# Projecting the last keys of four batches to V in three tiles

## The chip, the cores and the metric

The kernel runs on one core of a Trainium2 chip. Its measure is the device time of one execution in microseconds (us), as a median over runs. Five engines work side by side and wait for each other by semaphores: TensorE (PE in the rows; PEld is its weight load), VectorE (DVE), ScalarE (ACT), GpSimd (POOL) and SyncE (SP, which issues most of the DMAs).

## The reference, cut to what matters

Two layers of gated cross attention, each with a feed-forward part behind it. `ctx_1024` is the context, 8 batches of 722 keys of width 512; `x` has 8 batches of 100 queries. Both layers project the same context to K and V anew:

```python
def _heads(x):                       # 16 heads of 32
    b, s, _ = x.shape
    return x.reshape(b, s, H, W).transpose(0, 2, 1, 3)
q = _heads(x_q @ Wq.T + bq)
k = _heads(x_k @ Wk.T + bk)          # x_k = x_v = ctx_1024
v = _heads(x_v @ Wv.T + bv)
scores = jnp.einsum('bhqw,bhkw->bhqk', q, k) / np.sqrt(W)
...                                  # layer 0 masks keys, layer 1 does not
p = jax.nn.softmax(scores, axis=-1)
h = jnp.einsum('bhqk,bhkw->bhqw', p, v)
```

Layer 1 projects `h` once more by `Wo`. The feed-forward part of layer 0 has four ternary products, that of layer 1 is a quantized gate, up and down.

## The kernel before

**Precision.** Most operands are float32, split into a high part (a cast to `float32r`) and a low part (the rest), so a projection is three matmuls for each of the four blocks of 128 input features: high by high, low by high, high by low (`PAIRS`). Twelve matmuls make one *job*.

**Jobs.** A K job is a group of 128 output features (4 heads) over 384 or 338 keys: `("k", batch, group, half)`. A V job is a tile of 128 keys over all 512 output features: `("v", batch, kt)`. 722 keys are five tiles of 128 and one, `kt` = 5, of 82 rows. That last one is the V tail here.

**The attention loop.** `for i in range(NP)` runs over 64 pairs of heads, 8 for a batch. *Step i* on TensorE is: `scores(i+1)` (four matmuls), `turn(i)` (twelve transposes of the softmax weights), the jobs of `beside(i)`, then `weigh(i-1)`, six matmuls of weights by V. `BESIDE` sets which jobs go beside which of the 8 steps of a batch, mostly for the batch that follows; at i = 8b stand the V tail and the last K half of batch b itself.

**The others in step i.** ScalarE: `high_weighed(i-2)` (copies a part of a weighing out), `high_turned(i)` (three copies), the exponentials `weights(2i+2)` and `weights(2i+3)`, and `high_job`, which rounds a job's bank to the high part. The second exponential stands behind the first job where a step has two, and ahead of it where it has one (`len(beside(i)) < 2`). VectorE: two maxima (`peak`), `low_weighed(i-2)` (three additions), `low_turned(i)` (three subtractions), and `low_job`, which subtracts the high part from the bank. In layer 0 some steps are `early`: there `low_weighed` stands ahead of the maxima. GpSimd makes the low part of the next context (`low_ctx`); ScalarE makes the high part.

**Banks.** Jobs, weighings and a few more items (`inv`, `res`, `xn`, `out`) are written to PSUM banks 5 and 7 in turn. The list `RINGS` has the order; before item r is written, `ring_free` waits until item r-2 has been read: a job by `v_job` (its low part is made), a weighing by `v_fin` (its additions are done).

**K on its way.** High and low part of a K half are staged in `kst`, stored to DRAM (`store_k`) and loaded spread out over partitions (`load_k`). `high_job` of the K half waits until the staging tile of the group before has landed.

Of the kernel before, what the change touches and what calls it, by code (L numbers as in the profile page):

```python
# [6 lines left out]
F32R = mybir.dt.float32r  # L7
# [56 lines left out]
BESIDE = [(("v", 0, 5), ("k", 0, 3, 1)),  # L64
# [9 lines left out]
def beside(i):  # L74

    if i >= NP:
        return []
    return [(j[0], i // 8 + j[1]) + j[2:] for j in BESIDE[i % 8] if i // 8 + j[1] < B]

# [58 lines left out]
for _i in range(NP + 1):  # L138
    for _l in range(2):
        JOBS[_l] += beside(_i)  # L140
        if scaled_at(_i) is not None:
            RINGS[_l].append(("inv", scaled_at(_i)))
# [23 lines left out]
LAST_OF = {(j[1], half_of(j)): i for i, j in enumerate(JOBS[0])}  # L166
# [63 lines left out]
def flamingo_kernel(nc, t, out):  # L230
    top = ExitStack()
    with top:
# [28 lines left out]
        def scol(which, m):  # L261
# [13 lines left out]
        d_row, g_row = sem("d_row"), sem("g_row")  # L275
        d_xo = [sem(f"d_xo{b}") for b in range(B)]
# [24 lines left out]
        g_xf, g_ul, g_wh, g_mask, g_wl, g_rt, g_res, g_mv = (  # L301
            sem("g_" + n) for n in ("xf", "ul", "wh", "mask", "wl", "rt", "res", "mv"))
        g_self, g_nh, g_xr, g_wo, g_ol, g_rq, g_xn, g_xq = (
            sem("g_" + n) for n in ("self", "nh", "xr", "wo", "ol", "rq", "xn", "xq"))
# [15 lines left out]
        for L in range(2):  # L320
# [26 lines left out]
            x = 4 * TOKENS[L][0][1]  # L347
            m.xT = [PT[:, x * c:x * c + x].rearrange("p (k n) -> p k n", k=4) for c in (0, 1)]
# [83 lines left out]
        def job_out(m, j, bank):  # L432
            if j[0] == "k":
                return ps[:, bank, 0:HALF[j[3]][1]]
            return ps[0:KM[j[2]], bank, :]
# [69 lines left out]
        def _(e):  # L505
            w = Waits(e)
            def attention(L):
# [9 lines left out]
                if L == 0:  # L517
# [25 lines left out]
                    spread_q(L, m, 0)  # L543
                    store_k(L, m, *K30[1:])
                    load_ctx(L, m, 1, 0, 3)
                else:
# [22 lines left out]
                    load_k(L, m, 0, 1)  # L569
                    store_k(L, m, *K30[1:])  # L570
                for k in range(4):
                    load_ctx(L, m, 1, 1, k)
                for i in range(NP):
                    b, p = divmod(i, 8)
                    if p in (0, 2):
                        load_k(L, m, b, 2 + p // 2)
                    if L == 0 and p == 3 and b:
# [39 lines left out]
                    if p in (1, 5) and b + 2 < B:  # L617
                        for k in range(4):
# [42 lines left out]
            def load_ctx(L, m, b, half, k):  # L661
# [3 lines left out]
                e.dma_start(m.raw[:, k, off:off + n], t["ctx"][b, k][:, off:off + n]).then_inc(d_ctx[half][k], 16)  # L665

# [94 lines left out]
        def _(e):  # L761
# [13 lines left out]
            def attention(L):  # L775
# [31 lines left out]

                def ring_free(item):
# [1672 lines left out]
```

## Time and profile before

| | us |
|---|---|
| median of 3 runs (1589.46 to 1589.9) | 1589.48 |
| the profiled execution | 1587.91 |
| its span, first to last instruction | 1586.1 |
| TensorE busy | 1571.0 |
| VectorE busy | 1023.3 |
| ScalarE busy | 968.0 |
| GpSimd busy | 400.7 |

The two attention loops run from about 53 to 485 us (layer 0) and from 1056 to 1490 us (layer 1) of the span; between them lies the feed-forward part of layer 0, behind them that of layer 1. The page says how long each engine was busy; a chain of waits says which work ended last, step by step; a timeline has the instructions in order of time. A matmul's duration in a timeline overlaps the next one's, so the cost of a group is read from start to start.

### The profile page before, as it was taken

The page shows a single profiled execution, that of the slowest core. Times are in us where ns is not written, and L with a number is a line of the kernel's source. Part 1 is how long each engine was busy: PE and PEld are TensorE (multiplying, and loading weights), DVE is VectorE, ACT ScalarE, POOL GpSimd, SP SyncE. Part 2 cuts the span into 40 slices and gives each one's busy share as a digit, 9 for nine tenths or more (in the row PEclk, how much of TensorE's full clock was granted, in tenths as well). Part 3 has the DMA queues.
Part 4 walks back from the last instruction along what each step waited for, and adds up shares of the span by engine and source line. Part 5 has one row for each costly group of instructions (what it writes and reads, how often), then busy time and mean ns, then how long its engine had stood idle before and what let it go on. Part 6 is the DMA issues. An engine that isn't in the chain of part 4 may idle for free.

```text
span 1586.1 us, 25797 instructions
## 1 busy us (share of the span) xinstructions
PE 1571.0 (99%) x9370; PEld 1430.5 (90%) x9370; DVE 1023.3 (65%) x1821; ACT 968.0 (61%) x2006; POOL 400.7 (25%) x545
## 2 busy tenths in 40 slices
PE   9999999999999999999999999999999999999999
PEld 7899889989989999999999998889989989998765
DVE  6577787787785562223644425647777777777997
ACT  5666767677665455544544435457667667766676
POOL 4111211212144222222222222311102111113651
PEclk9999999999999999999999999999999999999999
DMA  8766776676572326554375643576676667658500
GB/s 245 181 170 169 184 188 178 156 202 175 144 206 86 104 80 198 175 186 160 108 229 194 220 154 98 177 176 180 153 195 165 162 178 178 178 128 227 179 13 30
DMA packets 146966, 258.15 MB, mean 163 GB/s; under 512 B 40944, under 2 KB 91248, under 8 KB 146701
## 3 DMA queue, kind: packets, MB, share of 16 engines
q1 hardware_dynamic: 146497, 256.10, 57.5%
q8 instruction: 86, 1.41, 0.4%
q14 instruction: 51, 0.42, 0.1%
q10 hardware_dynamic: 332, 0.23, 0.0%
HBM read 187.86 MB, written 58.57 MB: 155 GB/s over the span
## 4 chain that ended last, share of the span: by engine, by line
PE 92%; DVE 5%; ACT 2%; issue 1%; DMA 1%; SPq 0%; POOL 0%; DVEq 0%; ACTq 0%
PE ps L1148 33%; PE ps L802 17%; PE ps L798 15%; PE ps L884 8%; PE ps L862 8%; PE ps L950 2%; PE ps L1082 2%; PE ps L851 2%; PE ps L846 2%; PE ps L1099 1%; PE ps L849 1%; PE ps L850 1%; DVE PT L1295 1%; DVE nmax L1289 1%; ACT P L1806 1%
## 5 line engine op out<-in xcount | busy, mean ns | idle before, releaser
L1148 PE MATMUL ps<-ah_f,wh_f 128*128 128x400 f32 (+1 forms) x1296 | 442.9, 343 | 0.0
L1148 PE MATMUL ps<-al_f,wh_f 128*128 128x400 f32 (+1 forms) x1296 | 442.2, 342 | 0.0
L2165 POOL TENSOR_TENSOR cxl<-raw,cxh 128x384 fp32r<-128x384 f32 (+1 forms) x112 | 105.7, 965 | 613.5 <-ACT cxh L1763 613.5
L1685 DVE TENSOR_TENSOR wl_f<-raw_f,wh_f 128x1024 fp32r<-128x1024 f32 x85 | 103.7, 1223 | 232.4 <-POOL wh_f L2155 232.4
L1148 PEld LDWEIGHTS ps<-al_f,wh_f 128*128 128x128 f32 x1296 | 243.8, 188 | 0.0
L1148 PEld LDWEIGHTS ps<-ah_f,wh_f 128*128 128x128 f32 x1296 | 243.5, 188 | 0.1
L1289 DVE TENSOR_REDUCE nmax<-ps 100x1 f32<-100x722 f32 x256 | 220.7, 903 | 32.0 <-PE ps L850 28.6
L1806 ACT ACTIVATE P<-ps,nmax 100x722 f32<-100x722 f32 x256 | 219.9, 861 | 31.2 <-DVE nmax L1289 30.9
L1818 ACT ACTIVATE PT<-ps 128x400 fp32r<-128x400 f32 x384 | 165.9, 505 | 69.8 <-PE ps L862 68.5
L2083 ACT ACTIVATE raw_f<-wl_f 128x1024 f32<-128x1024 f32 x88 | 93.4, 1062 | 173.6 <-DVE wl_f L1685 173.6
L1295 DVE TENSOR_TENSOR PT<-ps,PT 128x400 fp32r<-128x400 f32 x384 | 196.4, 567 | 4.3 <-ACT PT L1818 1.1
L2155 POOL CAST wh_f<-raw_f 128x1024 fp32r<-128x1024 f32 x85 | 92.3, 1086 | 334.7 <-PE ps L1148 325.5
L798 PE MATMUL ps<-cxh,wkh 128*128 128x338 f32 (+1 forms) x512 | 172.0, 336 | 1.2 <-DVE cxl L1267 0.8
L798 PE MATMUL ps<-cxh,wkl 128*128 128x338 f32 (+1 forms) x512 | 167.8, 328 | 0.0
L798 PE MATMUL ps<-cxl,wkh 128*128 128x338 f32 (+1 forms) x512 | 167.0, 326 | 0.0
L802 PE MATMUL ps<-wvh,cxh 128*128 128x512 f32 (+1 forms) x384 | 159.1, 414 | 0.9 <-DVE V L1277 0.9
L862 PE MATMUL ps<-ident,P 100*128 100x100 f32 (+1 forms) x1536 | 152.9, 249 | 1.3 <-DVE PT L1295 1.3
L862 PEld LDWEIGHTS ps<-ident,P 100*128 100x128 f32 (+1 forms) x1536 | 143.0, 137 | 11.6 <-ACT P L1806 1.5
L884 PE MATMUL ps<-PT,V 128*128 128x400 f32 x720 | 151.0, 345 | 0.7 <-DVE ksl L1277 0.4
L802 PE MATMUL ps<-wvh,cxl 128*128 128x512 f32 (+1 forms) x384 | 151.1, 394 | 0.0
L802 PE MATMUL ps<-wvl,cxh 128*128 128x512 f32 (+1 forms) x384 | 150.7, 392 | 0.0
L1277 DVE SCALAR_TENSOR_TENSOR ksl<-ps,cols,ksh 128x384 fp32r<-128x384 f32 (+1 forms) x120 | 71.0, 592 | 112.1 <-ACT ksh L1774 112.0
(220 smaller groups left out, 2590.6 us busy)
## 6 DMA issues: line engine op xcount, KB each, us to landing
KS<-kd SPq DMA_DIRECT2D x192, 361.0 KB
raw_f<-in_h SPq DMA_DIRECT2D x64, 512.0 KB, 4.5
raw_f<-in_gud SPq DMA_DIRECT2D x48, 512.0 KB, 4.7
raw<-in_ctx SPq DMA_DIRECT2D x64, 192.0 KB, 3.9
raw_f<-in_w SPq DMA_DIRECT2D x24, 512.0 KB, 3.7
kd<-ksh SPq DMA_DIRECT2D x60, 192.0 KB, 2.1
kd<-ksl SPq DMA_DIRECT2D x60, 192.0 KB, 2.4
raw<-in_ctx SPq DMA_DIRECT2D x64, 169.0 KB, 4.3
```

Source lines behind the costliest of these rows:

```text
L798: ins = e.matmul(o, m.wk[x][:, k, 128 * j[2]:128 * j[2] + 128], m.cx[y][:, k, off:off + n], start=(k == 0 and c == 0), stop=(k == 3 and c ...
L802: ins = e.matmul(o, m.cx[y][:, k, 128 * kt:128 * kt + KM[kt]], m.wv[x][:, k, :], start=(k == 0 and c == 0), stop=(k == 3 and c == 2))
L862: ins = e.transpose(ps[0:KM[kt], bank, o:o + S], m.P[0:S, (2 * i + h) % 3, 128 * kt:128 * kt + KM[kt]], ident[0:S, 0:S])
L884: ins = e.matmul(o, m.V[b % 2][0:r, kt, g, 128 * pr:128 * pr + 128], m.PT[0:r, i % 2, :, kt, :], start=(kt == 0), stop=(kt == KT - 1))
L1148: return e.matmul(o, p, q, start=start, stop=stop)
L1289: e.tensor_reduce(m.nmax[0:S, c:c + 1], scores_of(n), AX.X, ALU.max, negate=True).then_inc(v_max, 1)
L1295: e.tensor_tensor(lo, ps[:, bank, 0:400].rearrange("p (k n) -> p k n", k=2), raw32(hi), ALU.subtract).then_inc(v_t, 1)
L1685: e.tensor_tensor(wl[:, z, :], raw[:, r, :], raw32(wh[:, z, :]), ALU.subtract).then_inc(v_ul, 1)
L1806: e.activation(m.P[0:S, n % 3, :], scores_of(n), ACT.Exp, bias=m.nmax[0:S, c:c + 1], accum_out=m.rs[0:S, r:r + 1]).then_inc(a_exp, 1)
L1818: e.activation(m.PT[:, i % 2, 0, 2 * x:2 * x + 2, :], ps[:, bank, 0:400].rearrange("p (k n) -> p k n", k=2), ACT.Copy).then_inc(a_t, 1)
L2083: e.activation(raw[:, r, :], raw32(wl[:, z, :]), ACT.Abs, accum_out=low[:, z, 0:1]).then_inc(a_raw, 1)
L2165: e.tensor_tensor(m.cx[1][:, k, off:off + n], m.raw[:, k, off:off + n], raw32(m.cx[0][:, k, off:off + n]), ALU.subtract).then_inc(g_cx, 1)
```

## The change

The V tails of batches 0, 1, 2, 3 have 4 x 82 = 328 rows. They are now put into three jobs, of 114, 128 and 114 rows, and those of batches 4 to 7 likewise: keys 0 to 81 of batch 0 and 64 to 81 of batch 1; keys 0 to 63 of batches 1 and 2; keys 64 to 81 of batch 2 and 0 to 81 of batch 3 (`PIECES`; the 18 rows stand at partition 96). The input for such a job is a new array, `ctxt`, that the host lays out (zeros where no key stands). It is loaded into a part of the tile of the raw context (for batch 0 elsewhere) and split to high and low by GpSimd (`split_tail`). The job of batches 0, 1, 2 (and 4, 5, 6) stands at step 8b behind `weigh(i-1)`; at steps 24 and 56 there is none. Its eviction is two pieces on ScalarE and two on VectorE in step 8b+1. `load_ctx(b+2)` of the first half now waits for the job.

```diff
-BESIDE = [(("v", 0, 5), ("k", 0, 3, 1)),
+BESIDE = [(("k", 0, 3, 1),),
...
+def tail_at(i):
+    return i // 8 if i < NP and i % 8 == 0 and i // 8 % 4 < 3 else None
+PIECES = (((0, 0, 0, 82), (96, 1, 64, 82)),
+          ((0, 0, 0, 64), (64, 1, 0, 64)),
+          ((96, 0, 64, 82), (0, 1, 0, 82)))
+TAIL_ROWS = (114, 128, 114)
...
+            JOBS[_l].append(("v", tail_at(_i), KT - 1))      # after beside(_i)
...
             RINGS[_l].append(("pv", _i - 1))
+        if tail_at(_i) is not None:
+            RINGS[_l].append(("v", tail_at(_i), KT - 1))
...
+            m.tail = [[x[:, k:k + 2, 0:256] for k in (2, 0)]
+                      for x in (at(f"tail{i}_{L}", place, shape, F32R) for i, (place, shape) in enumerate(ends))]
...
+                    if p == 7 and tail_at(i + 1) is not None:          # SyncE
+                        load_tail(L, m, b + 1)
...
                     if p in (1, 5) and b + 2 < B:
+                        if p == 1 and b:
+                            w.wait_ge(p_job, tail_done(L, b))
...
+            def load_tail(L, m, b):
+                if b:
+                    wait_ctx(w, L, b + 1, 0, 1)
+                else:
+                    w.wait_ge(p_xt, 8 * L + len(IN[L]))
+                e.dma_start(m.tail_raw[min(b, 1)], t["ctxt"][tail_of(b)].rearrange("p (a n) -> p a n", a=2)).then_inc(d_tail, 16)
...
+                def tail_job(b):                                        # TensorE
+                    j = ("v", b, KT - 1)
+                    ring_free(j)
+                    w.wait_ge(g_tail, 2 * (6 * L + tail_of(b)) + 2)
+                    r, o = TAIL_ROWS[b % 4], job_out(m, j, ring_bank(L, j))
+                    for k in range(4):
+                        wait_low_w(w, L, 4 + k)
+                        n = 128 * (k % 2)
+                        for c, (x, y) in enumerate(PAIRS):
+                            ins = e.matmul(o, m.tail[min(b, 1)][y][:, k // 2, n:n + r], m.wv[x][:, k, :],
+                                           start=(k == 0 and c == 0), stop=(k == 3 and c == 2))
+                    ins.then_inc(p_job, 1)
...
                     if i:
                         weigh(i - 1)
+                    if tail_at(i) is not None:
+                        tail_job(tail_at(i))
...
+                def low_tail(b):                                        # VectorE
+                    j = ("v", b, KT - 1)
+                    w.wait_ge(a_job, NJOB * L + JOB[L][j] + 1)
+                    for v, o in tail_parts(m, b, ring_bank(L, j)):
+                        ins = e.tensor_tensor(v[:, :, 1:3, :], o, raw32(v[:, :, 0:4:3, :]), ALU.subtract)
+                    ins.then_inc(v_job, 1)
...
                     if i >= 2 and not early and not between and (L == 0 or i < NP):
                         low_weighed(i - 2)
+                    if i and tail_at(i - 1) is not None:
+                        low_tail(tail_at(i - 1))
...
                     if i >= 2:                                          # ScalarE
                         high_weighed(i - 2)
+                    if i and tail_at(i - 1) is not None:
+                        high_tail(tail_at(i - 1))
...
+                def split_tail(b):                                      # GpSimd
+                    (high, low), new = m.tail[min(b, 1)], m.tail_raw[min(b, 1)]
+                    w.wait_ge(d_tail, 16 * (6 * L + tail_of(b) + 1))
+                    if b:
+                        wait_ctx(w, L, b + 1, 0, 3)
+                    e.tensor_copy(high, new).then_inc(g_tail, 1)
+                    w.wait_ge(g_tail, 2 * (6 * L + tail_of(b)) + 1)
+                    e.tensor_tensor(low, new, raw32(high), ALU.subtract).then_inc(g_tail, 1)
```

TensorE, layer 1, batch 1: from the end of the K half in step 8 (L798, after it L848) into step 9, before. L884 and L948 are the weighing, L846 to L851 and L910 to L915 the scores, L862 and L926 the transposes, L802 and L852 the V projection of the next batch, L868 the tail's job:

```order
L798 MATMUL ps<-cxh_74,wkl_84 128x338
L884 MATMUL ps<-PT_89,V_1_85 128x400 x6
L846 MATMUL ps<-KS_91,QS_88 100x512
L849 MATMUL ps<-KS_91,QS_88 100x210
L850 MATMUL ps<-KS_91,QS_88 100x210
L851 MATMUL ps<-KS_91,QS_88 100x512
L862 MATMUL ps<-ident,P_78 128x100 x10
L862 MATMUL ps<-ident,P_78 82x100 x2
L802 MATMUL ps<-wvh_76,cxh_74 128x512
```

and with the change:

```order
L848 MATMUL ps<-cxh_78,wkl_88 128x338
L948 MATMUL ps<-PT_93,V_1_89 128x400 x6
L868 MATMUL ps<-wvh_80,tail_1_103 128x512 x2
L868 MATMUL ps<-wvl_81,tail_1_103 128x512
L868 MATMUL ps<-wvh_80,tail_1_103 128x512 x2
L868 MATMUL ps<-wvl_81,tail_1_103 128x512
L868 MATMUL ps<-wvh_80,tail_1_103 128x512 x2
L868 MATMUL ps<-wvl_81,tail_1_103 128x512
L868 MATMUL ps<-wvh_80,tail_1_103 128x512 x2
L868 MATMUL ps<-wvl_81,tail_1_103 128x512
L910 MATMUL ps<-KS_95,QS_92 100x512
L913 MATMUL ps<-KS_95,QS_92 100x210
```

The tail came in behind the weighing and ahead of the scores. What the next V projection waits for, at its first matmul, before:

```order
L862 MATMUL ps<-ident,P_78 128x100 [waits v_t]
L862 MATMUL ps<-ident,P_78 128x100
L862 MATMUL ps<-ident,P_78 82x100 x2
L802 MATMUL ps<-wvh_76,cxh_74 128x512 [waits g_cx,v_job]
L802 MATMUL ps<-wvh_76,cxl_75 128x512
```

and with the change:

```order
L926 MATMUL ps<-ident,P_82 128x100 [waits v_t]
L926 MATMUL ps<-ident,P_82 128x100
L926 MATMUL ps<-ident,P_82 82x100 x2
L852 MATMUL ps<-wvh_80,cxh_78 128x512 [waits g_cx,v_fin]
L852 MATMUL ps<-wvh_80,cxl_79 128x512
```

`v_job` (a job's low part) has become `v_fin` (the additions of a weighing). ScalarE in step 8 of the same batch and the start of step 9, before. `sum` is `high_weighed`, `PT` is `high_turned`, `P,rs` an exponential, `V` and `ksh` the evictions of a V job and a K half:

```order
L1833 ACTIVATE sum_90<-ps 64x200 [waits v_fin,p_pv]
L1818 ACTIVATE PT_89<-ps 128x2x200 [waits p_t] x3
L1806 ACTIVATE P_78,rs_81<-ps,nmax_82 100x722 [waits v_max]
L1787 ACTIVATE V_1_86<-ps 82x4x2x64 [waits p_job]
L1806 ACTIVATE P_78,rs_81<-ps,nmax_82 100x722
L1774 ACTIVATE ksh_96<-ps,cols 128x338 [waits d_kd12,p_job]
L1833 ACTIVATE sum_90<-ps 64x200 [waits v_fin,p_pv]
```

and with the change:

```order
L1924 ACTIVATE sum_94<-ps 64x200 [waits v_fin,p_pv]
L1909 ACTIVATE PT_93<-ps 128x2x200 [waits p_t] x3
L1897 ACTIVATE P_82,rs_85<-ps,nmax_86 100x722 [waits v_max]
L1897 ACTIVATE P_82,rs_85<-ps,nmax_86 100x722
L1850 ACTIVATE ksh_100<-ps,cols 128x338 [waits d_kd12,p_job]
L1924 ACTIVATE sum_94<-ps 64x200 [waits v_fin,p_pv]
L1878 ACTIVATE V_1_89<-ps 18x4x2x64 [waits p_job]
L1878 ACTIVATE V_1_90<-ps 82x4x2x64
```

The K half's eviction now stands behind both exponentials, and the tail's two pieces ahead of the copies of step 9. VectorE, the end of step 8 and step 9, before. `nmax` is a maximum, `sum` and `QT` the additions of a weighing, `PT` the three subtractions, `ksl` and `V` low parts:

```order
L1295 TENSOR_TENSOR PT_89<-ps,PT_89 128x2x200 [waits a_t] x3
L1281 TENSOR_TENSOR V_1_86<-ps,V_1_86 82x4x128 [waits a_job]
L1277 SCALAR_TENSOR_TENSOR ksl_97<-ps,cols,ksh_96 128x338 [waits a_job]
L1289 TENSOR_REDUCE nmax_82<-ps 100x1 [waits a_exp,p_sc] x2
L1310 TENSOR_TENSOR sum_90<-ps,sum_90 64x200 [waits a_pv]
L1314 TENSOR_TENSOR QT_93<-ps,sum_90 32x100 [waits v_self]
L1314 TENSOR_TENSOR QT_93<-ps,sum_90 32x100
L1295 TENSOR_TENSOR PT_89<-ps,PT_89 128x2x200 [waits a_t] x3
```

and with the change:

```order
L1369 TENSOR_TENSOR PT_93<-ps,PT_93 128x2x200 [waits a_t] x3
L1343 SCALAR_TENSOR_TENSOR ksl_101<-ps,cols,ksh_100 128x338 [waits a_job]
L1363 TENSOR_REDUCE nmax_86<-ps 100x1 [waits a_exp,p_sc] x2
L1384 TENSOR_TENSOR sum_94<-ps,sum_94 64x200 [waits a_pv]
L1388 TENSOR_TENSOR QT_97<-ps,sum_94 32x100 [waits v_self]
L1388 TENSOR_TENSOR QT_97<-ps,sum_94 32x100
L1355 TENSOR_TENSOR V_1_89<-ps,V_1_89 18x4x128 [waits a_job]
L1355 TENSOR_TENSOR V_1_90<-ps,V_1_90 82x4x128
L1369 TENSOR_TENSOR PT_93<-ps,PT_93 128x2x200 [waits a_t] x3
```

The tail's two low parts stand behind the maxima and the additions.

## Rows read from the trace of the kernel before

**Rows 1.** Page before, parts 1 and 2: TensorE busy, its granted clock
```profile
PE 1571.0 (99%) x9370; PEld 1430.5 (90%) x9370; DVE 1023.3 (65%) x1821; ACT 968.0 (61%) x2006; POOL 400.7 (25%) x545
...
PEclk9999999999999999999999999999999999999999
```

**Rows 2.** Waits of TensorE: who, for whom, us, times, longest
```profile
PE ps L802 <- DVE V L1277: 0.9, 1, 0.9
```

**Rows 3.** Chain of waits, layer 1, steps 8 and 9: start, us, what
```profile
1117.74 2.77 PE ps L802 x12
1120.51 1.86 PE ps L798 x12
1122.38 1.09 PE ps L884 x6
...
1125.15 2.80 PE ps L802 x12
```

**Rows 4.** Timeline, layer 1, TensorE: start, us, engine, line, operation, out<-in
```profile
1115.89 0.40 PE L846 MATMUL ps<-KS,QS 96*100 96x512 f32 x1
...
1123.31 0.39 PE L846 MATMUL ps<-KS,QS 96*100 96x512 f32 x1
...
1124.93 0.48 PE L802 MATMUL ps<-wvh,cxh 128*128 128x512 f32 x1
```

**Rows 5.** The same timeline, ScalarE
```profile
1118.28 0.86 ACT L1806 ACTIVATE P<-ps,nmax 100x722 f32<-100x722 f32 x1
...
1122.41 0.54 ACT L1774 ACTIVATE ksh<-ps,cols 128x338 fp32r<-128x338 f32 x1 [0.43 <-PE ps L798]
...
1125.69 0.87 ACT L1806 ACTIVATE P<-ps,nmax 100x722 f32<-100x722 f32 x1
...
1127.29 0.20 ACT L1806 ACTIVATION_READ_ACCUMULATOR P<-ps,nmax 100x1 f32 x1
```

**Rows 6.** The same timeline, VectorE
```profile
1116.52 1.73 DVE L1289 TENSOR_REDUCE nmax<-ps 100x1 f32<-100x722 f32 x2
1118.16 0.35 DVE L1310 TENSOR_TENSOR sum<-ps,sum 64x200 f32<-64x200 f32 x1
...
1119.13 1.54 DVE L1295 TENSOR_TENSOR PT<-ps,PT 128x400 fp32r<-128x400 f32 x3
1121.18 0.69 DVE L1281 TENSOR_TENSOR V<-ps,V 82x512 fp32r<-82x512 f32 x1 [0.51 <-ACT V L1787]
1122.99 0.57 DVE L1277 SCALAR_TENSOR_TENSOR ksl<-ps,cols,ksh 128x338 fp32r<-128x338 f32 x1 [1.13 <-ACT ksh L1774]
...
1126.09 0.54 DVE L1314 TENSOR_TENSOR QT<-ps,sum 32x100 f32<-32x100 f32 x2
```

**Rows 7.** Timelines, TensorE, two weighings: without a wait, after one
```profile
1122.21 1.25 PE L884 MATMUL ps<-PT,V 128*128 128x400 f32 x6
...
211.12 1.36 PE L884 MATMUL ps<-PT,V 128*128 128x400 f32 x6 [0.39 <-DVE ksl L1277]
```

**Rows 8.** Groups by line, GpSimd: xcount | busy us, mean ns | idle before
```profile
L2186 POOL TENSOR_TENSOR wol<-wos,woh 128x512 fp32r<-128x512 f32 x4 | 5.0, 1282 | 0.1
...
L2183 POOL CAST woh<-wos 128x512 fp32r<-128x512 f32 x4 | 2.3, 615 | 7.1 <-PE ps L802 7.1
```

**Rows 9.** Timeline of layer 1, step 8: GpSimd and the queue of SyncE
```profile
1115.07 1.99 POOL L2165 TENSOR_TENSOR cxl<-raw,cxh 128x384 fp32r<-128x384 f32 x2 [4.46 <-ACT cxh L1763]
...
1119.07 1.27 SPq L693 DMA_DIRECT2D KS<-kd  x3
```

**Rows 10.** Timeline, layer 0, step 33, TensorE
```profile
289.45 0.39 PE L846 MATMUL ps<-KS,QS 98*100 98x512 f32 x1
...
291.43 0.47 PE L802 MATMUL ps<-wvh,cxh 128*128 128x512 f32 x1
```

**Rows 11.** Timeline, layer 0, step 56, VectorE
```profile
455.38 0.54 DVE L1409 TENSOR_SCALAR x<-x,mv,rq 100x512 f32<-100x512 f32 x1
```

**Rows 12.** Chain of waits in order of time, layer 0, step 57
```profile
458.76 0.91 DVE nmax L1289
```

More of the change, by code:

```diff
@@ L151 @@
             RINGS[_l].append(("pv", _i - 1))
+        if tail_at(_i) is not None:
+            RINGS[_l].append(("v", tail_at(_i), KT - 1))
 for _l in range(2):
@@ L162, in half_of @@
     return j[3] if j[0] == "k" else j[2] // 3
-LAST_OF = {(j[1], half_of(j)): i for i, j in enumerate(JOBS[0])}
+LAST_OF = {(j[1], half_of(j)): i for i, j in enumerate(JOBS[0]) if j[0] == "k" or j[2] < KT - 1}
 PLACES = [{i: r for r, i in enumerate(ring)} for ring in RINGS]
@@ L300, in flamingo_kernel @@
         g_ones, g_cx, g_ql, g_rx, g_low, g_tot = (sem("g_" + n) for n in ("ones", "cx", "ql", "rx", "low", "tot"))
[L301 to L304, printed above, removed]
+        g_xf, g_ul, g_wh, g_mask, g_wl, g_rt, g_res, g_set = (
+            sem("g_" + n) for n in ("xf", "ul", "wh", "mask", "wl", "rt", "res", "set"))
+        g_self, g_xr, g_wo, g_ol, g_rq, g_xn, g_xq = (
+            sem("g_" + n) for n in ("self", "xr", "wo", "ol", "rq", "xn", "xq"))
         base = -(-nc.sbuf_base // 32) * 32
@@ L347, in flamingo_kernel @@
             x = 4 * TOKENS[L][0][1]
+            ends = [(o["V1"] + 16384, [128, 4, 256]), (o["raw"], [128, 4, T])]
+            m.tail = [[x[:, k:k + 2, 0:256] for k in (2, 0)]
+                      for x in (at(f"tail{i}_{L}", place, shape, F32R) for i, (place, shape) in enumerate(ends))]
+            m.tail_raw = [at(f"traw{i}_{L}", place, shape)[:, 0:2, 0:256] for i, (place, shape) in enumerate(ends)]
             m.xT = [PT[:, x * c:x * c + x].rearrange("p (k n) -> p k n", k=4) for c in (0, 1)]
@@ L434, in job_out @@
                 return ps[:, bank, 0:HALF[j[3]][1]]
-            return ps[0:KM[j[2]], bank, :]
+            return ps[0:TAIL_ROWS[j[1] % 4] if j[2] == KT - 1 else KM[j[2]], bank, :]
         def ring_bank(L, item):
@@ L474, in rows_of, with tail_done, tail_parts @@
             return x.rearrange("b s d -> (b s) d")[ROW0[n]:ROW0[n] + ROWS[n], :]
+        def tail_done(L, b):
+            return NJOB * L + JOB[L]["v", b - (b % 4 == 3), KT - 1] + 1
+        def tail_parts(m, b, bank):
+            return [(m.V[(b + x) % 2][r0:r1, KT - 1, :, :].rearrange("p g (r n) -> p g r n", r=4),
+                     ps[o:o + r1 - r0, bank, :].rearrange("p (g r n) -> p g r n", g=4, r=2)) for o, x, r0, r1 in PIECES[b % 4]]
         def high_columns(m, j):
@@ L1788, in high_job, with high_tail @@
                                      ACT.Copy).then_inc(a_job, 1)
+                def high_tail(b):
+                    j = ("v", b, KT - 1)
+                    w.wait_ge(p_job, NJOB * L + JOB[L][j] + 1)
+                    w.wait_ge(p_pv, NP * L + 8 * b)
+                    if b == 0:
+                        w.wait_ge(p_xt, 8 * L + len(IN[L]))
+                        w.wait_ge(p_q, 8 * L + 8)
+                        for g in (1, 2):
+                            for h in range(2):
+                                w.wait_ge(d_kd[h][g], kd_done(L, g))
+                    for v, o in tail_parts(m, b, ring_bank(L, j)):
+                        ins = e.activation(v[:, :, 0:4:3, :], o, ACT.Copy)
+                    ins.then_inc(a_job, 1)
                 def high_q(b):
@@ L2341, in attention @@
                     b, p = divmod(i, 8)
+                    if i and tail_at(i) is not None:
+                        split_tail(b)
                     if scaled_at(i + 1) is not None:
@@ L2442, in col @@
         return v.reshape(-1, 128).T
+    tails = np.zeros((6, 128, 4, 128), np.float32)
+    for b in range(B):
+        for o, x, r0, r1 in PIECES[b % 4] if b % 4 < 3 else ():
+            keys = I["ctx_1024"][b + x, 640 + r0:640 + r1, :]
+            tails[tail_of(b), :, :, o:o + r1 - r0] = keys.reshape(r1 - r0, 4, 128).transpose(2, 1, 0)
+    tails = tails.reshape(6, 128, 512)
     a = {
@@ L2446 @@
         "ctx": I["ctx_1024"].transpose(0, 2, 1).reshape(B, 4, 128, T),
+        "ctxt": tails,
         "mask": I["mask_BxS2_ik0"],
```

21 lines of the change are left out of this document (14 added, 7 removed).

## The prediction

> **What bounds the kernel now.** I read the page first: its busy line has TensorE at 99% of the span, and the clock line is full in all forty slices [rows 1]. So a matmul that goes is worth its time, provided that nothing else makes TensorE wait, and a wait that comes is paid in full. The table of waits comes next: projections of context (L802) waited 0.9 us in all the run, once [rows 2]. There is no slack for a gain to hide in. Then the chain of waits in order of time, for what one step of the attention loop is made of. I call step i what TensorE does between the first score matmul of pair i+1 and that of pair i+2; in layer 1, batch 1, step 8 begins at 1115.89 and step 9 at 1123.31 [rows 4]. In step 8 the chain shows the V tail 2.77, the K half 1.86 and the weighing 1.09 [rows 3]; scores and transposes stand before them, and the first job of a step starts 1.62 into it (1124.93 less 1123.31) [rows 4]. The timelines of ScalarE and VectorE come last, because the eviction of a PSUM bank goes through both, and the two banks 5 and 7 are handed out in turn.
>
> **What is removed.** A V projection is twelve matmuls of 512 columns, whether it has 82 or 128 rows: 2.77 against 2.80 [rows 3]. Each layer has eight V tails before and six after (none at steps 24 and 56), so four go: 4 x 2.80 = 11.2 us. Rows 96 to 113 or 64 to 127 of the tile cost TensorE nothing by these two rows.
>
> **What is added off the path.** Twelve loads of 256 KB, a cast and a subtraction of 512 elements on GpSimd each: 0.62 + 1.28 us [rows 8]. GpSimd ends its subtraction for the context at 1117.06 [rows 9], 1.17 into step 8, so the split would end at 3.1. If both took double, because of the strided view, it would be 5.0; TensorE wants it at about 5.4 (below). The load is put into the queue when GpSimd has done the pair before, 4.46 us before 1115.07 [rows 9], and its bytes have nearly six microseconds. I take nothing for it. ScalarE and VectorE get 24 evictions for 16, and they have time: the cost lies in where they stand. The queue of SP is moved too: its load of context b+2 at step 8b+1 now waits for the tail on TensorE, about 8.3 us into step 8b, and behind it stand loads of keys that are used five steps later; nothing.
>
> **What is moved: the first new wait.** Before, step 8b had two jobs, V tail and K half, then the weighing. Now it has the K half, the weighing, and then the tail, which takes the bank that the K half held. TensorE: K half from 1.62 to 3.48, weighing to 4.57. ScalarE: with one job in a step both exponentials stand ahead of the job's eviction. The first begins at 2.39 (1118.28), and the second and its accumulator end 1.80 after such a start (1125.69 to 1127.49), where the next eviction may start about 0.1 earlier [rows 5]: the K eviction runs from 4.1 to 4.6. VectorE has its three subtractions until 4.78 and then the K part of 0.57 [rows 6]: 5.35. With 0.05 for the semaphore the tail can start at 5.40, not 4.57: 0.83. A restart costs more: the weighing that had to wait shows 1.36, one that had not 1.25 [rows 7], so 0.11. First wait 0.94. The second half of the K block before must have landed in DRAM as well, for the staging tile is used again: SP's load that waits for it went out at 1119.07, 3.18 into the step [rows 9], ahead of 4.1, so nothing.
>
> **The second new wait.** The next projection, V of batch b+1 in step 8b+1, takes the bank of weighing 8b-1, which before it did not: there it took that of the K half. VectorE frees this bank by the additions of weighing 8b-1, and they stand in step 8b+1 behind its two maxima. The maxima cannot start before the scores of that step, and these come after the tail. In step 9 the additions ended at 1126.63, 3.32 into the step, and TensorE wants to start the projection at 1.62 [rows 4, 6]. With 0.05 and the restart of 0.11: 3.37 - 1.62 + 0.11 = 1.86. This holds for the five middle places of layer 1 and for batch 1 of layer 0. In layer 0 from batch 2 on, the additions come ahead of the maxima and one more item takes a bank; then the projection wants the bank of the tail, whose two low parts stand behind the maxima. Maxima done at 2.27 (1118.16 less 1115.89; the next begins then), two parts of 0.69 that overlap by 0.05: 3.60; the projection wanted 1.98 (291.43 less 289.45) [rows 6, 10]. 3.65 - 1.98 + 0.11 = 1.78.
>
> **The sum.** Places: batches 1, 2, 4, 5, 6 in two layers, ten. Batch 0 has no weighing ahead and its next projection takes the bank of the K half, so I count nothing there. First waits 10 x 0.94 = 9.4; second waits 6 x 1.86 + 4 x 1.78 = 18.3; together 27.7. From the 11.2 I take what is late next. Step 56 without its tail is 4.6 long: in layer 0 VectorE then has the three subtractions to 4.78, a normalization of 0.54 and K's 0.57 [rows 6, 11], so 5.87, where the maxima could start at 5.23 (0.63 after the scores' start, 1116.52 less 1115.89): 0.6 lost, since from 458.76 on the chain runs over VectorE [rows 12]. Layer 1, without the normalization: 0.1. In layer 0 batch 3, step 25, the additions now start late and the projection with them: 0.3. So 11.2 - 0.6 - 0.1 - 0.3 = 10.2 is left. 27.7 - 10.2 = +17.5 us. The profiled execution took 1587.91, 1.8 more than its span of 1586.1; with the change 1605.4. The median of the runs is 1.57 above that execution: 1607.0.
>
> **Bounds of what is not shown.** A bank wait of this form is not in the trace of before. From below: the first wait could vanish (the K eviction is ready at 3.7, were it taken between the exponentials), which leaves 18.3 - 10.2 = +8.1. From above: each restart as dear as the first matmuls after a wait in the trace, some 0.3 in place of 0.11, and a late landing of the keys: +5, so +22.5. An eviction of 18 partitions lies between nothing and the 0.69 of 82; at nothing the four places of layer 0 would win 0.64 each, -2.6; were it double, +2.8. I take the full 0.69, since the rows of 82 and of 128 partitions agree [rows 6].
>
> A page of the Trainium skill speaks against this change in another way: "TensorE: Matmul & The Clock Gate", section "A second HAM failure mode: psum-queue depth-cycling", says that a TensorE that idles briefly between groups of matmuls, as it cycles through PSUM banks, can swing between its half and its full clock. By that rule the twenty new pauses would also slow what follows them. The row of the trace has the full 2.4 GHz in every slice [rows 1], though with hardly a pause in it, so it cannot decide.
>
> **Rivals.** (A) The waits do not come: the additions and the K part are done in time, so that TensorE finds both banks free. Place: steps 8b and 8b+1; price 0; then -10.2, and the time is 1579.3, faster. It decides for this if the bank of weighing 8b-1 is free at 1.6 into step 8b+1. For it speaks that TensorE waited so little until now; against it the order of VectorE, in which nothing can move the additions ahead of the maxima. Chance 0.09. (B) Only one kind of wait is paid: with the first alone 9.4 - 10.2, 1588.7, no change (0.03); with the second alone +8.1, 1597.6 (0.08). (C) The input of the tail is late at GpSimd or in the queue: TensorE waits for it beyond 5.4; were it 1 us at ten places, 1617.0. The room of 2.3 us speaks against it. Chance 0.06. (D) The clock drops to 1.2 GHz in the pauses. Were one projection of 2.80 after each of ten places at half speed, that is +28: 1635.0. Chance 0.03. The forecast keeps 0.71.
>
> **Numbers.** A measurement here can tell 0.2%, 3.2 us, from no change. Slower: 0.71 + 0.08 + 0.06 + 0.03 = 0.88; same 0.03; faster 0.09. Forecast 1607.0, its own range 1601 to 1612 by the bounds; down to 1597 to take in the second kind alone, up to 1614 for part of (C).
>
> **What would show it.** In the profile after: the idle time before the first matmul of a tail about 0.8 us, ended by VectorE's K part (L1343); before the projection of step 8b+1 about 1.8 us, ended in layer 1 by the additions (L1388), in layer 0 from batch 2 on by the low tail (L1355); steps 8b and 8b+1 together 15.8 us in layer 1 where they were 13.0; steps 24 and 56 shortened to about 4.6; TensorE at 97%. The forecast is wrong if TensorE shows none of these, or if step 24 is not shorter, or if the split on GpSimd ends later than 5.4.

## The result and the profile after

The median went from 1589.47 us to 1609.03 us (1608.46 to 1609.52): a ratio of 1.0123, with a 95% interval of 1.0111 to 1.0135. The change made the kernel 19.6 us slower, where 17.5 were forecast. The profiled execution took 1608.54 us, with a span of 1606.1; it stands against 1587.91 and 1586.1 before. The first lines of the page after:

```profile
PE 1567.9 (98%) x9322; PEld 1430.4 (89%) x9322; DVE 1027.6 (64%) x1829; ACT 970.4 (60%) x2014; POOL 423.9 (26%) x569
...
PE 85%; DVE 8%; issue 2%; DMA 2%; ACT 1%; SPq 1%; POOL 0%; DVEq 0%; ACTq 0%
```

48 matmuls fewer, four tails of twelve, and TensorE's busy time fell by 3.1 us only, while the span grew by 20 [rows 1]. The second line is the chain that ended last: VectorE's share in it is 8%, where it was 5% before. The table of TensorE's waits names the place, where before the projections (now L852, then L802) had waited 0.9 us [rows 2]. Its columns are engine, line and releaser, then us in all, times, the longest:

```profile
PE ps L852 <- DVE QT L1388: 9.2, 6, 1.5
PE ps L852 <- DVE V L1355: 6.5, 4, 1.6
PE ps L868 <- DVE ksl L1343: 4.7, 10, 0.5
PE ps L1063 <- POOL otl L2294: 1.8, 2, 1.6
```

The first three rows came six, four and ten times, each with the releaser that the prediction named: 20.4 us of idle. The steps of the same twenty places grow by more, 25.9 us (table below): a matmul's end in the profile is modelled, so that a part of each wait counts as busy, and a tail takes a little longer in its new place (see the first wait, below). The timeline of layer 1, batch 1, shows both waits. Step 8 begins at 1127.93 and step 9 at 1136.10. First the engines that free the bank of the K half, then the tail (L868), then step 9:

```profile
1131.16 0.86 ACT L1897 ACTIVATE P<-ps,nmax 100x722 f32<-100x722 f32 x1
...
1131.51 1.25 PE L948 MATMUL ps<-PT,V 128*128 128x400 f32 x6
...
1132.00 0.54 ACT L1850 ACTIVATE ksh<-ps,cols 128x338 fp32r<-128x338 f32 x1
1132.61 0.56 DVE L1343 SCALAR_TENSOR_TENSOR ksl<-ps,cols,ksh 128x338 fp32r<-128x338 f32 x1
...
1133.23 0.73 PE L868 MATMUL ps<-wvh,tail 128*128 128x512 f32 x2 [0.47 <-DVE ksl L1343]
...
1136.10 0.39 PE L910 MATMUL ps<-KS,QS 96*100 96x512 f32 x1
...
1136.73 1.72 DVE L1363 TENSOR_REDUCE nmax<-ps 100x1 f32<-100x722 f32 x2 [3.56 <-PE ps L914]
...
1138.89 0.54 DVE L1388 TENSOR_TENSOR QT<-ps,sum 32x100 f32<-32x100 f32 x2
...
1139.46 1.39 DVE L1355 TENSOR_TENSOR V<-ps,V 64x512 fp32r<-64x512 f32 x2
1139.49 0.50 PE L852 MATMUL ps<-wvh,cxh 128*128 128x512 f32 x1 [1.52 <-DVE QT L1388]
```

ScalarE's K eviction starts 4.07 us into the step, behind the second exponential; VectorE's K part ends at 5.24; the tail starts at 5.30. In step 9 the maxima start after the scores, the additions behind them end at 1139.43, and the projection starts 3.39 into the step. Before it stood at 1.62 [rows 4].

Lengths of the steps (from the first score matmul of one pair to that of the next, in the timelines of TensorE) show where the time went, in us:

| steps | before | after | each | times | sum |
|---|---|---|---|---|---|
| 24 and 56 (tail gone), both layers | 7.43 | 4.69 | -2.74 | 4 | -11.0 |
| 8b with a tail | 7.43 | 8.19 | +0.77 | 10 | +7.7 |
| 8b+1, layer 1, and step 9 of layer 0 | 5.59 | 7.36 | +1.77 | 6 | +10.6 |
| 17, 33, 41, 49 of layer 0: the wait | 5.93 | 7.82 | +1.89 | 4 | +7.6 |
| of these 17 and 41: the clock | | 9.35 | +1.53 | 2 | +3.1 |
| step 1, both layers | 6.14 | 5.59 | -0.55 | 2 | -1.1 |
| steps from 57 on, both layers | | | | | +3.4 |
| the rest | | | | | -0.3 |

That is +20.0, the difference of the spans. The fifth row, the clock, was not in the forecast. In step 17 of layer 0 (TensorE from 179.00, the projection after its wait):

```profile
179.00 0.39 PE L910 MATMUL ps<-KS,QS 98*100 98x512 f32 x1
...
181.38 1.40 DVE L1355 TENSOR_TENSOR V<-ps,V 18x512 fp32r<-18x512 f32 x2
...
182.84 0.70 PE L852 MATMUL ps<-wvh,cxh 128*128 128x512 f32 x1 [1.64 <-DVE V L1355]
183.33 0.63 PE L852 MATMUL ps<-wvh,cxl 128*128 128x512 f32 x1
183.41 0.22 ACT L1897 ACTIVATION_READ_ACCUMULATOR P<-ps,nmax 100x1 f32 x1
183.76 0.63 PE L852 MATMUL ps<-wvl,cxh 128*128 128x512 f32 x1
```

The matmuls start 0.43 us apart, and 0.23 in step 9 of layer 1. The windows over the same place (stretch; its length, TensorE's busy us and instructions; granted clock; DMA share, GB/s):

```profile
179.00:182.80 3.80, 2.20 (x21) 1.00 1.05 310
182.80:186.20 3.40, 3.37 (x8) 0.52 0.20 69
186.20:188.40 2.20, 2.20 (x12) 0.96 0.00 0
```

The granted clock was 0.52 for 3.4 us, which is the level of 1.2 GHz of the two (the window's edge takes in a little of the other): it fell 0.1 us after TensorE took up work behind the pause of 1.64. The same came in step 41, there 0.5 us after the pause. In the trace of before there is one such stretch only, in the last microseconds.

### The profile page after: what moved, and what is told of

The parts are those of the page before. It is cut to its first block, busy times and chain, and to the rows that moved or that the text cites. A ratio compares the mean times of both kernels' runs of the same rounds, so it can differ in the third digit from the quotient of the medians.

```text
span 1606.1 us, 25776 instructions
## 1 busy us (share of the span) xinstructions
PE 1567.9 (98%) x9322; PEld 1430.4 (89%) x9322; DVE 1027.6 (64%) x1829; ACT 970.4 (60%) x2014; POOL 423.9 (26%) x569
## 4 chain that ended last, share of the span: by engine, by line
PE 85%; DVE 8%; issue 2%; DMA 2%; ACT 1%; SPq 1%; POOL 0%; DVEq 0%; ACTq 0%
PE ps L1214 32%; PE ps L852 14%; PE ps L848 13%; PE ps L948 7%; PE ps L926 6%; PE ps L868 2%; PE ps L1014 2%; PE ps L1148 2%; PE ps L910 2%; DVE PT L1369 2%; DVE nmax L1363 2%; PE ps L915 1%; PE ps L1165 1%; PE ps L914 1%; PE ps L913 1%
## 5 line engine op out<-in xcount | busy, mean ns | idle before, releaser
L848 PE MATMUL ps<-cxh,wkh 128*128 128x338 f32 (+1 forms) x512 | 173.3, 339 | 1.1 <-DVE cxl L1333 0.6
L848 PE MATMUL ps<-cxh,wkl 128*128 128x338 f32 (+1 forms) x512 | 167.9, 328 | 0.0
L848 PE MATMUL ps<-cxl,wkh 128*128 128x338 f32 (+1 forms) x512 | 167.0, 326 | 0.0
L926 PE MATMUL ps<-ident,P 100*128 100x100 f32 (+1 forms) x1536 | 152.9, 249 | 1.3 <-DVE PT L1369 1.3
L926 PEld LDWEIGHTS ps<-ident,P 100*128 100x128 f32 (+1 forms) x1536 | 143.1, 137 | 11.6 <-ACT P L1897 1.5
L948 PE MATMUL ps<-PT,V 128*128 128x400 f32 x720 | 151.0, 345 | 0.6 <-DVE ksl L1343 0.6
L852 PE MATMUL ps<-wvh,cxh 128*128 128x512 f32 x320 | 134.0, 419 | 16.6 <-DVE QT L1388 9.2
L948 PEld LDWEIGHTS ps<-PT,V 128*128 128x128 f32 x720 | 130.3, 188 | 4.0 <-DVE ksl L1343 1.1
L852 PE MATMUL ps<-wvh,cxl 128*128 128x512 f32 x320 | 127.3, 398 | 0.0
```

What stands on the lines that cost most here:

```text
L848: ins = e.matmul(o, m.wk[x][:, k, 128 * j[2]:128 * j[2] + 128], m.cx[y][:, k, off:off + n], start=(k == 0 and c == 0), stop=(k == 3 and c ...
L852: ins = e.matmul(o, m.cx[y][:, k, 128 * kt:128 * kt + KM[kt]], m.wv[x][:, k, :], start=(k == 0 and c == 0), stop=(k == 3 and c == 2))
L926: ins = e.transpose(ps[0:KM[kt], bank, o:o + S], m.P[0:S, (2 * i + h) % 3, 128 * kt:128 * kt + KM[kt]], ident[0:S, 0:S])
L948: ins = e.matmul(o, m.V[b % 2][0:r, kt, g, 128 * pr:128 * pr + 128], m.PT[0:r, i % 2, :, kt, :], start=(kt == 0), stop=(kt == KT - 1))
```

## The experiments

My theory was that the whole loss is the two waits for banks 5 and 7, set by VectorE's order. The rivals were the copies themselves (twice as many, in two pieces), the input of the tail at GpSimd, and the clock. The first four kernels each move one thing, the third on top of the first.

**Additions ahead of the maxima.** VectorE evicts the weighing 8b-1 ahead of the maxima in every step 8b+1, as it did already in four places of layer 0:

```
-                    early = scaled_at(i) is not None or L == 0 and i < NP - 7 and (
+                    early = scaled_at(i) is not None or i >= 2 and tail_at(i - 1) is not None or L == 0 and i < NP - 7 and (
```

> Against the changed kernel (1609.0 us): in step 8b+1 VectorE makes the three additions of weighing 8b-1 before the two maxima, also in layer 1 and for batch 1 of layer 0 (layer 0 from batch 2 on has this order already). Theory (TensorE pays for two bank waits): the second wait, 1.5 us of idle at each of six places and 1.77 of step length, goes, since VectorE stands idle for 2 to 3.5 us before the scores of that step; 6 x 1.77 = 10.6 less, 1598.4 us. The four waits of layer 0 that VectorE's low tail ends stay, and so does any fall of the clock there. Rival (the eight more evictions load ScalarE and VectorE; their order is no matter): no change, 1609. Rival (the input of the tail is late): no change.

Measured: 1597.12 us (1596.52 to 1598.3), against before 1.0049 (1.0036 to 1.0063). The six steps 8b+1 are back at 5.60, and the waits of TensorE read

```profile
PE ps L852 <- DVE V L1355: 6.5, 4, 1.6
PE ps L868 <- DVE ksl L1343: 4.7, 10, 0.5
```

The row of L1388 is gone, and so are about 12 of the 20 us, 10.6 of them in the six steps. The second wait in these six places is VectorE's order, as the prediction had it.

**K eviction between the exponentials.** ScalarE takes the K half ahead of its second exponential in the steps with a tail:

```
+                    if tail_at(i) is not None:
+                        high_job(beside(i)[0])
                     if len(beside(i)) < 2 and i + 1 < NP:
                         weights(2 * i + 3)
...
                     for j in beside(i)[:1]:
-                        high_job(j)
+                        if tail_at(i) is None:
+                            high_job(j)
```

> ScalarE evicts the K half in steps 8b before its second exponential instead of behind it. If ScalarE's place of that eviction sets the first wait (0.47 us of idle, 0.77 of step length, ten places), up to 7.7 us go: 1601. Theory: VectorE ends its three subtractions 4.7 us into the step, when ScalarE is done in either order, so the tail still starts at 5.3 and nothing moves: 1609.0, within 1 us.

Measured: 1608.78 us (1607.88 to 1612.49), 1.0129 (1.0114 to 1.0145): nothing gained, steps 8b still 8.19. The bound from below of the prediction ("the K eviction is ready at 3.7") took this for a way out. It is none. In layer 0, step 16, which begins at 171.39, ScalarE now evicts the K half from 3.81 to 4.35 us into the step, but VectorE's three subtractions of the turned P stand ahead of its K part, which begins at 4.70 all the same, and the tail at 5.32:

```profile
174.64 1.54 DVE L1369 TENSOR_TENSOR PT<-ps,PT 128x400 fp32r<-128x400 f32 x3
...
175.20 0.54 ACT L1850 ACTIVATE ksh<-ps,cols 128x338 fp32r<-128x338 f32 x1 [0.45 <-PE ps L848]
...
176.09 0.56 DVE L1343 SCALAR_TENSOR_TENSOR ksl<-ps,cols,ksh 128x338 fp32r<-128x338 f32 x1
...
176.71 0.72 PE L868 MATMUL ps<-wvh,tail 128*114 128x512 f32 x2 [0.45 <-DVE ksl L1343]
```

**The tail's low part ahead of the maxima.** The kernel with the additions moved, and in layer 0 from batch 2 on VectorE subtracts the tail ahead of the maxima too:

```
+                    ahead = L == 0 and i > 16 and tail_at(i - 1) is not None
+                    if ahead:
+                        low_tail(tail_at(i - 1))
...
-                    if i and tail_at(i - 1) is not None:
+                    if i and tail_at(i - 1) is not None and not ahead:
                         low_tail(tail_at(i - 1))
```

> As the kernel with the additions first, and in layer 0 from batch 2 on (steps 17, 33, 41, 49) VectorE makes the two low parts of the tail before the maxima. Theory: TensorE's wait there falls from 1.64 us of idle to about 0.3 (ScalarE's two pieces end 1.3 into the step, the low parts about 2.1, and the projection wants its bank at 1.98), so 4 x 1.5 = 6 less, and the two stretches at 1.2 GHz in steps 17 and 41, 1.55 us each, go as well: 1598.4 - 6 - 3.1 = 1589.3. If the clock falls whatever the wait, 1592.4. Rival (load, not order): 1609.

Measured: 1591.40 us (1590.15 to 1593.33), 1.0015 (1.0006 to 1.0024). Steps 17, 33, 41 and 49 are all 6.86 (7.82 or 9.35 in the changed kernel). The waits are

```profile
PE ps L868 <- DVE ksl L1343: 4.7, 10, 0.5
PE ps L852 <- DVE V L1355: 2.7, 4, 0.7
```

The clock did not fall in layer 0's loop; it fell once, in step 61 of layer 1 (8.99 us long), behind a wait of 1.65 for GpSimd's low part of the output. Of the bank waits the first is left, with 0.7 in four places where 0.3 was expected: the kernel is 2 us behind before, though 11 us of matmuls are gone.

**The tail behind the next scores.** TensorE computes the tail in step 8b+1, after the scores, so that VectorE's maxima no longer wait for it:

```
                         scores(i + 1)
+                    if i and tail_at(i - 1) is not None:
+                        tail_job(tail_at(i - 1))
                     turn(i)
...
-                    if tail_at(i) is not None:
-                        tail_job(tail_at(i))
```

> TensorE does the tail in step 8b+1 behind the scores and ahead of the transposes, in place of at the end of step 8b; nothing else is moved. Theory: the maxima no longer stand behind the tail; the scores fill most of the first wait (bank free at 5.3, scores done at 5.2), and the bank of weighing 8b-1 is free at about 8.0 where the next projection wants it at 9.2. First wait 0.2 at ten places, second none at six places and about 0.8 at the four of layer 0: 2 + 3.2 against 10.2 to 11.3 gained: 1583.5 us, below the kernel before. Rival (load of ScalarE and VectorE, or a late input): no change, 1609.

Measured: 1590.59 us (1588.33 to 1592.94), 1.0010 (1.0001 to 1.0019): 7 us short of the expectation. Steps 8b and 8b+1 of layer 1 together take 13.11 us (15.55 in the changed kernel, 13.0 before), as expected. Three things were missed. For batch 0 the pair of steps takes 13.25 and not 11.93, 1.3 in each layer: there no wait was to be won, and the scores of step 1, with no tail ahead of them, now wait for the exponentials (0.5 and 0.3 us). Steps 57 and 58 of layer 1 are 2.2 longer together: a wait of 1.27 for an exponential, and behind it, in step 58, 3.4 us at a granted clock of 0.50. And in the four late places of layer 0 the projection still waits:

```profile
PE ps L852 <- DVE V L1355: 5.4, 4, 1.3
PE ps L910 <- ACT P L1897: 2.8, 4, 1.3
```

Here the projection takes the very bank of the tail, and between the two lie only the transposes of P (1.2 us) and those of the normalised rows (0.5 us). The second row is the scores that wait for an exponential (1.3 us in all, two times, in the changed kernel).

**Every bank left alone long enough.** So the next kernel chooses for each place. Batch 0 as in the changed kernel, the others as in the last one, but for the four late places: there the transposes of the normalised rows, the tail, the projection and the weighing take the banks in this order, so that a whole projection lies between the tail and the next user of its bank:

```
                         turn_normal(turned_at(i))
+                    if behind_normal(L, i):
+                        tail_job(tail_at(i - 1))
                     for j in beside(i):
```

The cut shows the four late places alone. With it go the order of the banks (`RINGS`), ScalarE's copy of that tail between its two exponentials, and VectorE's subtraction behind the turned P.

> The six tails of V are kept as in the changed kernel, but placed so that each of the two banks has long been free when TensorE comes to it. Batch 0: where it was. Batches from 1 on, but for layer 0's steps 17, 33, 41 and 49: behind the scores of step 8b+1, ahead of the turning of P (as in e5_behind_scores: steps 8b and 8b+1 together 13.1 us, where they were 15.6 in the changed kernel and 13.0 before the change). In layer 0's steps 17, 33, 41 and 49: behind the turning of the normalised rows and ahead of the projection of V, so that the tail follows the weighing's bank, the projection follows the bank of the turned rows (0.5 us of ScalarE), and the next weighing follows the tail's bank a projection of 2.8 us later; ScalarE copies the tail between its two exponentials, VectorE subtracts behind the turned P. Theory (the whole loss of the change is waits for the two banks): these four steps fall from 8.43 + 1.9 of e5 to about 8.7, steps 16 and 17 together to 13.4 to 13.7; against e5 that is 4 x 1.5 = 6 less, and 2 x 1.3 less for batch 0, no fall of the clock in layer 0: 1590.6 - 6 - 2.6 = 1582, 0.5% faster than before the change. Rival (the chain of copies, not the banks, is what costs: VectorE and ScalarE have more to do beside each tail in its two pieces): the wait comes again at the next weighing or at the exponentials, and the time stays at that of e5, 1590.

Measured: 1582.13 us (1581.03 to 1582.89), against before 0.9955 (0.9941 to 0.9968): 6.9 us faster than before the change and 27 faster than the changed kernel, with the same six tails, the same copies and the same loads. Steps 16 and 17 of layer 0 take 4.70 and 9.00, as expected; the pair is 0.35 longer than before the change, and in layer 1 the pairs are 0.1 longer. TensorE's waits hold none of the three. Its first rows are the output projection, a product of the feed-forward part and scores:

```profile
PE ps L1070 <- POOL otl L2309: 1.7, 2, 1.6
PE ps L1159 <- DVE hb L1692: 1.6, 3, 1.1
PE ps L920 <- ACT P L1910: 1.4, 4, 0.4
```

In step 17 TensorE goes from the tail (L875) into the projection (L859) and on to the weighing (L955) almost without a pause, while the copies follow:

```profile
178.21 0.40 PE L875 MATMUL ps<-wvl,tail 128*114 128x512 f32 x1
178.45 0.39 PE L859 MATMUL ps<-wvh,cxh 128*128 128x512 f32 x1
178.65 1.20 ACT L1891 ACTIVATE V<-ps 18x512 fp32r<-18x512 f32 x2 [0.39 <-PE ps L875]
...
179.87 1.39 DVE L1366 TENSOR_TENSOR V<-ps,V 18x512 fp32r<-18x512 f32 x2 [1.04 <-ACT V L1891]
...
181.00 0.39 PE L859 MATMUL ps<-wvl,cxh 128*128 128x512 f32 x1
181.32 1.36 PE L955 MATMUL ps<-PT,V 128*128 128x400 f32 x6
```

The clock stays at its full level through both loops. The rival, that the copies are the cost, is out: they are all there, and the 27 us are gone.

**One tail more.** Batches 0 to 3 keep tails of their own; 4 to 7 stay merged:

```
-    return i // 8 if i < NP and i % 8 == 0 and i // 8 % 4 < 3 else None
+    return i // 8 if i < NP and i % 8 == 0 and i // 8 < 7 else None
...
+PIECES = (((0, 0, 0, 82),),) * 4 + PIECES
```

> The first four batches keep a tail of 82 rows of their own (four tiles, at steps 0, 8, 16 and 24), the last four are merged into three as before. One tail more in each layer, and the tails of steps 0 to 24 are copied in one piece and not two. Theory: in layer 1 step 24 goes from 4.68 to 8.2 (2.75 of matmuls, 0.77 of wait for the K half's bank) and step 25 from 5.58 to 7.36 (the wait for the weighing's bank, ended by L1388's subtraction, whatever the pieces): +5.3. In layer 0 step 24 likewise +3.5; but at 17 and 25, where the wait is for the tail's own bank, the one piece saves 0.6 on ScalarE and 0.7 on VectorE: a wait of about 0.5 and not 1.6 to 1.9, so step 25 +0.5 and step 17 -1.3, and a fall of the clock less (1.5): about +1.2 to +2.7. Sum +6.5 to +8: 1615.5 to 1617. Rival (a tail costs only its matmuls, the waits come from elsewhere): 2 x 2.75 = 5.5, 1614.5 with steps 25 unchanged.

Measured: 1614.57 us (1613.16 to 1615.92), 1.0159 (1.0145 to 1.0173). By steps: 24 of layer 1 8.14, 25 7.36, as expected; 24 of layer 0 8.17, 25 7.10 (+1.07 where 0.5 was expected) and 17 7.10. The fall of the clock that I expected to go did not in the profiled execution: it has two as the changed kernel's, now in steps 33 and 49 of layer 0. Steps 59 to 61 of layer 1, which the expectation left alone, became 1.3 shorter together. The median is 1 us under the expectation, the profiled execution (1615.91, mean clock 0.998) within it; the others of the five have mean clocks of 0.998 to 1.000, so some had fewer falls. The total alone does not tell the theory from the rival at 1614.5; step 25 does, as the rival has it unchanged.

**A longer second wait.** VectorE subtracts the tail ahead of the additions in the six places where it stood behind:

```
+                    if i and tail_at(i - 1) is not None:
+                        low_tail(tail_at(i - 1))
                     if i >= 2 and not early and not between and (L == 0 or i < NP):
                         low_weighed(i - 2)
-                    if i and tail_at(i - 1) is not None:
-                        low_tail(tail_at(i - 1))
```

> On VectorE the subtraction of the tail goes ahead of that of the weighing in the six places where it stood behind it (layer 1's steps 9, 17, 33, 41 and 49, layer 0's step 9). The bank that the projection of V waits for comes free 1.4 us later. Theory (the second wait is this bank, one to one): these six steps go from 7.36 to about 8.75, +1.35 x 6 = +8.1: 1617.1, and the clock falls where it happens to, once or twice in all. Rival (the wait is hidden elsewhere, or its price is that of the clock): no longer step, 1609; or a wait of 3 us brings the clock down each time, 1.55 us in each of six places more: 1626.

Measured: 1624.33 us (1621.59 to 1627.90), 1.0221 (1.0207 to 1.0235), between theory and rival. Of the six steps two are 8.66 and 8.82, 1.29 and 1.44 longer: the price of the wait, one to one. The other four are 10.22, 10.38, 11.36 and 11.36, and there the clock fell. In the profiled execution the six steps grew by 16.6 us together: 8.2 of wait, at 1.37 each, and 8.4 of clock. Layer 1, step 33, the projection in the timeline of TensorE:

```profile
1318.57 0.79 PE L852 MATMUL ps<-wvh,cxh 128*128 128x512 f32 x1 [2.84 <-DVE QT L1388]
1319.16 0.63 PE L852 MATMUL ps<-wvh,cxl 128*128 128x512 f32 x1
```

The windows over it, with columns as above:

```profile
1317.60:1320.60 3.00, 2.03 (x5) 0.50 0.26 89
1320.60:1323.60 3.00, 3.00 (x9) 0.50 0.00 0
```

The clock was at 1.2 GHz over all these 6 us, from a microsecond before the projection on, that is, from within the pause. So a pause has a second price, not paid each time. Three more falls of this execution stand at waits that were not lengthened: in steps 33 and 49 of layer 0, and in step 58 of layer 1 behind a wait of 1.0 for an exponential.

**The input later.** GpSimd makes the cast of the tail four times:

```
+                    for _ in range(3):
+                        me.then(e.tensor_copy(high, new))
+                        me.settle()
                     e.tensor_copy(high, new).then_inc(g_tail, 1)
```

> GpSimd makes the cast of the tail's input four times and not once: the split of it ends 1.95 us later, about 5.25 us into step 8b, where the bank that the tail waits for comes free 5.3 us into it. Theory (the first wait is that of the bank, and the input laid out for the tail is early by 2 us): no change, 1609.0 (1608.5 to 1610). Rival (the input is what ends the wait, or is just in time): each of ten places 1.95 later, 1628, and the waits of the tail's matmuls are ended by GpSimd.

Measured: 1614.40 us (1611.30 to 1616.49), 1.0154 (1.0138 to 1.0169). I expected no change and was wrong, though not by the rival's 19 us. In layer 0, step 16 (from 171.10), GpSimd's subtraction ended at 176.43, 5.33 into the step, and VectorE's K part at 176.36:

```profile
175.15 1.28 POOL L2272 TENSOR_TENSOR tail<-traw,tail 128x512 fp32r<-128x512 f32 x1
...
175.80 0.56 DVE L1343 SCALAR_TENSOR_TENSOR ksl<-ps,cols,ksh 128x338 fp32r<-128x338 f32 x1
...
176.57 0.69 PE L868 MATMUL ps<-wvh,tail 128*114 128x512 f32 x2 [0.60 <-POOL tail L2272]
```

So the input came just behind the bank: steps 8b are 8.32 and not 8.19 (+1.3 in ten), and step 0 of layer 1 is 1.45 longer. This accounts for 2.8 us. The other 4.6 of the profiled execution are the clock: five falls in the loops where the changed kernel has two, at about 1.55 each. None of the five follows one of the lengthened pauses: they stand behind waits of 1.5 to 1.6 that the changed kernel has too (steps 17, 33 and 49 of layer 0, 49 and 61 of layer 1). Nor is five a fixed number. The mean granted clock of the four executions on record is 0.995 to 0.997, that of the changed kernel's four 0.998, and the two slower ones of the four have the two lower clocks (0.995 and 0.996, against 0.997 twice). The room for the input in the changed kernel is a little under 2 us (3.3 against 5.3); I had reckoned 2.3.

## Why the prediction was right

**The four tails.** The forecast had 11.2 us gone; measured are 11.0 (2.74 each). A tile costs TensorE the same with 82 rows as with 114 or 128, as rows 3 had it.

**The first wait.** Forecast 0.94, measured 0.77, ten times. The chain of copies was right link by link: K eviction at 4.07 for 4.1, K part done at 5.24 for 5.35, tail at 5.30 for 5.40; the 0.05 for the semaphore is 0.06. Two terms of the sum were off. TensorE could have started the tail at 4.68, where step 24 ends, and not at 4.57, so the wait itself is 0.62 and not 0.83. And the 0.11 for a restart, from one weighing [rows 7], is not there: the tail takes 2.88 behind the wait, and 2.88 also where it has no wait (step 9 of layer 1 in the kernel with the tail behind the scores). But 2.88 is 0.14 more than the 2.74 that a tail gave back at step 24, and 0.62 and 0.14 are the 0.77. That the total came near is in part luck.

**The second wait.** Forecast 1.86 in six places, measured 1.77: the additions end 3.33 into the step for 3.32, and again the 0.11 is not there (the projection takes 2.88 to the weighing, 2.86 before). Forecast 1.78 in four places, measured 1.89: the tail's two subtractions end 3.78 into the step for 3.60. They last the whole 1.4 us, though the first has 18 partitions, so that bound is settled at the full price. Both kinds together: forecast 27.7, measured 25.9.

**Late next.** Step 57 of layer 0 lost 0.9 for the 0.6 forecast (whose parts add up to 5.89 and not 5.87), step 25 0.1 for 0.3. Not forecast were 0.8 in step 59 of layer 0 and 1.65 in steps 59 to 61 of layer 1. There TensorE waited 1.57 for GpSimd's low part of the output (L2294), where before it had waited 0.56. With four tails left in the first half (seven in a layer) these three steps are 5.58, 5.94 and 6.72, close to before (5.59, 5.92 and 6.35). Which link shifts with the number of tails was not tested.

**Step 1**, counted at nothing, became 0.55 shorter in each layer. Before, its projection waited there twice for GpSimd's split of the context (L2165), which waits for ScalarE; the tail's eviction no longer stands ahead of ScalarE's part, which begins 1.04 us ahead of step 1 (1079.28 to 1080.32) and not 0.33 (1067.41 to 1067.74). The table of waits, in which the prediction read a single wait of the projections [rows 2], does not hold these two: they lie inside the modelled durations, and show only from start to start (0.39 and 0.40 us between two matmuls in place of 0.23).

**The clock.** Rival D had 0.03 and a fall in each of ten places. It came in two of ten, 3.1 us. The sum forecast was 17.5 and the profiled executions differ by 20.6. The waits came 1.8 and step 1 came 1.1 under the forecast, the clock 3.1 and the steps 59 to 61 of both layers 2.5 over it, smaller items 0.4. So 2.9 us of errors one way stand against 6.0 the other way, and that the sum came as near as 3.1 was in part luck. Rivals A and B are out by the table of waits, and C by the releasers of the tail, which are VectorE in all ten.

The Trainium skill's rule ("TensorE: Matmul & The Clock Gate", section "A second HAM failure mode: psum-queue depth-cycling") is borne out in kind: before, with hardly a pause, the clock stayed full through both loops; with twenty pauses it fell twice; with six of them lengthened to 3.0 us it fell seven times, four of them in those six places; and in the fastest kernel, without the twenty, not at all. As a price for each pause it would be far too high here, as 18 of the 20 passed at 2.4 GHz.

## What to carry to other kernels

When a job moves behind another, write down for both PSUM banks who evicts them, on which engine, and behind what: the matmuls saved (11 us) were worth less than two banks that came free late and made ten pairs of steps 2.6 us longer each. Put the users of a bank apart by a whole job of TensorE, place by place, as the places differ in their order; the same change then wins 0.45% in place of losing 1.2%. Here a pause of TensorE cost its length at least, and where there were many of 1.5 us and more, some falls of the clock, at about 1.5 us each, stood on top.

## What the hardware showed that I had not expected

Behind a pause, or within a long one, the granted clock fell in single places, at a cost of 1.5 us or so each. It was not bound to the place: in the changed kernel steps 17 and 41 of layer 0, with the additions moved steps 33 and 49, with the K eviction moved step 41 alone, after waits of the same length (1.6). The five waits of 1.5 in layer 1 of the changed kernel brought none; with the input later one of the same five did (step 49). Waits of 3.0 us brought more falls and longer ones: four in six places, two of them of 6.8 us. A wait of 1.6 for the output's low part in step 61 of layer 1 brought a fall in two kernels and none in others, the changed and the fastest one among them, and a wait of 1.0 to 1.3 in step 58 brought one in two. All places are of one profiled execution for each kernel, and the mean clocks show that the number of falls differs between executions of one kernel (0.990 to 0.994 with the longer second wait, 1621.6 us at the highest and 1627.9 us at the lowest clock). What decides between two equal pauses is left open.
